# A four-layer graph network on one core: in the last layer, rows at run ends picked by one-hot products beside the groups, instead of a store of all rows and a second gather

## The reference, cut to what matters

```python
def _L3_gnn_ref(x, weight, bias, src, dst, rel):
    x_src = x[src]
    msg = zeros
    for r in range(4):
        hr = x_src @ weight[r] + bias[r]
        msg = where((rel == r)[:, None], hr, msg)
    agg = segment_max(msg, dst, num_segments=6250)
    agg = where((deg > 0)[:, None], agg, 0)
    return x @ weight[-1] + bias[-1] + agg

x = _layernorm(x + _L3_gnn_ref(x, ...))
```

## Time and profile before

| | |
|---|---|
| median of 3 runs | 4120.34 us |
| the profiled execution | 4121.19 us |
| its span, first to last instruction | 4119.4 us |
| PE / weight load busy in the span | 2465.8 / 2169.4 us |
| VectorE busy | 2245.0 us |
| ScalarE busy | 1038.2 us |
| POOL busy | 2912.2 us |
| granted TensorE clock, mean of the span | 0.632 of full speed |
| DMA | 602.65 MB, 147 GB/s over the span |

### The profile page before, as it was taken

How to read it: one execution, slowest core, us unless ns; L and a number is a source line. 1 busy time by engine, 2 the same in 40 slices (tenths; PEclk the granted TensorE clock), 3 DMA queues, 4 the chain that set the end, 5 groups by cost and what they waited for, 6 DMA issues and landing times. The chain is left out here.

```text
span 4119.4 us, 67476 instructions
## 1 busy us (share of the span) xinstructions
PE 2465.8 (60%) x18096; PEld 2169.4 (53%) x18096; DVE 2245.0 (54%) x6458; ACT 1038.2 (25%) x2890; POOL 2912.2 (71%) x3009
## 2 busy tenths in 40 slices
PE   2566666676647777529999977777633333333330
PEld 2454555454436666529999976666523333333330
DVE  5777777777744444436767668876522222222224
ACT  0244454444410111114444411111111111111112
POOL 2777777777747777626777777777377777777775
PEclk8555655656658898655555557767756556555655
DMA  4344444444425666446666678787545455444443
GB/s 121 97 113 129 116 132 128 117 130 115 130 71 144 146 147 147 80 95 176 183 182 176 185 217 262 249 246 250 178 122 130 129 134 132 129 132 132 130 129 94
DMA packets 454541, 602.65 MB, mean 146 GB/s; under 512 B 112602, under 2 KB 322350, under 8 KB 451086
## 3 DMA queue, kind: packets, MB, share of 16 engines
q1 hardware_dynamic: 344578, 392.09, 31.1%
q0 software_dynamic: 95744, 198.37, 22.2%
q10 hardware_dynamic: 14000, 9.82, 0.8%
HBM read 420.34 MB, written 184.16 MB: 147 GB/s over the span
## 5 line engine op out<-in xcount | busy, mean ns | idle before, releaser
L628 POOL DMA_INDIRECT G<-table,IC x2096 | 2002.2, 955 | 743.7 <-issue 633.3
L3342 DVE TENSOR_TENSOR_SCAN GW<-BIG,GW,PS 128x512 f32<-128x512 bf16 x208 | 266.2, 1280 | 781.6 <-PE PS L3317 766.8
L3317 PE MATMUL PS<-IDENT,G 128*128 128x128 f32 x832 | 204.2, 427 | 679.3 <-DMA G<-table,IC 679.3
L2936 POOL DMA_INDIRECT G<-table,IC x448 | 465.6, 1039 | 196.4 <-issue 139.0
L3317 PEld LDWEIGHTS PS<-IDENT,G 128*128 128x128 f32 x832 | 162.8, 223 | 717.7 <-DMA G<-table,IC 520.7
L2936 POOL DMA_INDIRECT G<-table2c,IC x384 | 369.8, 963 | 123.5 <-issue 116.2
L1284 PE MATMUL PS<-SEL,GW 128*128 128x96 f32 x1664 | 371.7, 414 | 78.1 <-DVEq L1360 78.1
L1284 PEld LDWEIGHTS PS<-SEL,GW 128*128 128x128 f32 x1664 | 347.2, 318 | 118.2 <-DVEq L1360 118.2
L2950 PE MATMUL PS<-BIG 128*128 128x49 f32 x1680 | 377.5, 412 | 1.1 <-ACT BIG L2885 1.1
L2950 PEld LDWEIGHTS PS<-BIG 128*128 128x128 f32 x1680 | 371.3, 333 | 1.3 <-ACT BIG L2885 1.3
L1162 ACT CAST BIG<-PS 128x490 bf16<-128x490 f32 x288 | 199.8, 706 | 257.1 <-PE PS L1149 252.4
(11 more groups left out here) (378 smaller groups left out, 4525.7 us busy)
## 6 DMA issues: line engine op xcount, KB each, us to landing
rows_ahead<-G SPq DMA_DIRECT2D x104, 520.0 KB
running_max<-BIG SPq DMA_DIRECT2D x105, 512.0 KB
GW<-source_in_block SPq DMA_DIRECT2D x160, 256.0 KB
G<-table,IC POOLq DMA_INDIRECT x2544
SCRATCH<-rows_ahead SPq DMA_DIRECT2D x78, 520.0 KB
SCRATCH<-edge_places SPq DMA_DIRECT2D x209, 192.0 KB
edge_counts<-BIG SPq DMA_DIRECT2D x24, 1568.0 KB
BIG<-run_mask SPq DMA_DIRECT2D x104, 256.0 KB
```

The source lines that it names most:

```text
L628: pool.indirect_dma_start(out=G[:, b, u, 0:width], out_offset=None, in_=table, in_offset=bass.IndirectOffsetOnAxis(ap=IC[:, b * U + u:b * ...
L2936: pool.indirect_dma_start(out=GS[:, b, u, 0:width], out_offset=None, in_=table, in_offset=bass.IndirectOffsetOnAxis(ap=IC[:, b * U + u:b * ...
L3317: last = t.transpose(PS[2 * q + u // 4][:, (u % 4) * P:(u % 4 + 1) * P], G[:, b, u, 0:D], IDENT[:])
L3342: v.tensor_tensor_scan(RM[:, q, h * 512:(h + 1) * 512], MB[:, q, h * 512:(h + 1) * 512], PS[2 * q + h][:], before, ALU.min, ALU.max).then_ ...
```

## The change

`edges3` and `finish` get a branch: they run only where `FLAG[0:1, 8:9]` is above 0 (`not_counted`). A new stage at the very end, `edges3_ends`, runs where it is below 1. The order of stages is now ..., rest2, edges3, exact3, finish, edges3_ends. The new stage has its loops written out for all 104 groups, but for POOL's, which stays a loop of 26 turns with the same gathers. For a group i:

- the gathers, transposes in, the scan, transposes back and the copies to RB are as before; RUNS is neither written nor read;
- VectorE compares `IOTA` with ENDREL (line 3624 of the new kernel): the edge's place in its window if it is the last edge of its run, else -1;
- TensorE multiplies: for each of the 8 tiles RB (edges x 128 features) by SEL (edges x 96), summed in PS6, so that each column is the one row at the end of that node's run (line 3588);
- VectorE adds the window to ACC (line 3646). Nodes without edges stay 0;
- at i = 12, 16, ..., 100 two node blocks are turned from ACC (line 3597), added to X and HS, and normalised over the next groups; SP stores them to `out`. The last 3 blocks follow the last group.

ENDREL comes ahead of the first group: SP loads the mask shifted by one edge, VectorE takes RELROW + 1 where the next edge starts a run, TensorE turns the 7 tiles of it, VectorE subtracts 1 and clears ACC (128 x 6368).

```diff
         def edges3():
...
                 @block.gpsimd
                 def _(pool):
+                    with pool.If(not_counted(pool)):
...
+        def edges3_ends():
...
+            def event(i, later):
+                n = (i - later) // RING - FIRST
+                return n if (i - later) % RING == 0 and 0 <= n < CHUNKS else None
...
+                def load_mask(sp, i):
+                    if i >= 2:
+                        sp.wait_ge(scanned, i - 1)
+                    sp.dma_start(MB[:, i % 2, :], MASKD[i * L:(i + 1) * L].unsqueeze(0)
+                                 .to_broadcast([P, L])).then_inc(mask_in[i % 2], 16)
...
+                def copy_back(act, i):
+                    q = i % 2
+                    act.wait_ge(back, i + 1)
+                    if i >= 2:
+                        act.wait_ge(picked, i - 1)
+                    a.copy(RB[:, q, 0:4, :], PS[4][:].rearrange("p (u f) -> p u f", u=4))
+                    a.copy(RB[:, q, 4:8, :], PS[5][:].rearrange("p (u f) -> p u f", u=4)).then_inc(copied, 1)
...
+                        for i in range(GROUPS + 1):
+                            if i < GROUPS:
+                                b = i % RING
+                                act.wait_ge(turned, i + 1)
+                                a.copy(IC[:, b * U:(b + 1) * U],
+                                       IDX3[:, (i + RING) * U:(i + RING + 1) * U]).then_inc(ic_ready, 1)
+                            if i >= 1:
+                                copy_back(act, i - 1)
+                            if event(i, 1) is not None:
+                                spread(act, event(i, 1))
+                            if event(i, 2) is not None:
+                                write_out(act, event(i, 2))
...
+                def turn_in(pe, i):
+                    b, q = i % RING, i % 2
+                    pe.wait_ge(gathered[b], i // RING * (16 * U) + 16 * U)
+                    if i >= 2:
+                        pe.wait_ge(scanned, i - 1)
...
+                def pick(pe, i):
+                    q = i % 2
+                    pe.wait_ge(copied, i + 1)
+                    pe.wait_ge(sel_ready, i + 1)
+                    if i >= 1:
+                        pe.wait_ge(added, i)
+                    for u in range(U):
+                        last = t.matmul(PS[6][:, 0:W], RB[:, q, u, :], SEL[:, q, u, :], start=u == 0, stop=u == U - 1)
+                    last.then_inc(picked, 1)
...
+                            if i < GROUPS:
+                                turn_in(pe, i)
+                            if i >= 1:
+                                turn_back(pe, i - 1)
+                            if i < GROUPS and event(i, 0) is not None:
+                                turn_nodes(pe, event(i, 0), i - 1)
+                            if i >= 1:
+                                pick(pe, i - 1)
+                        turn_nodes(pe, CHUNKS, GROUPS)
...
+                def select_ends(dve, i):
+                    if i >= 2:
+                        dve.wait_ge(picked, i - 1)
+                    v.tensor_tensor(SEL[:, i % 2], times(IOTA[:, 0:W], U), per(ENDREL[:, i * U:(i + 1) * U], W),
+                                    ALU.is_equal).then_inc(sel_ready, 1)
...
+                def mix_best(dve, cn, n):
+                    b0, nb = events[n]
+                    Y = X[:, b0:b0 + nb, :]
+                    dve.wait_ge(sums_turned, n + 1)
+                    cn.step(v.tensor_tensor(Y, rows(PS[7], nb), Y, ALU.add))
+                    dve.sem_inc(taken, 1)
+                    cn.step(v.tensor_tensor(Y, Y, HS[:, b0:b0 + nb, :], ALU.add))
...
+                        for i in range(GROUPS + 1):
+                            if event(i, 2) is not None:
+                                scale(dve, event(i, 2))
+                            if i < GROUPS:
+                                dve.reg_load([regs[i % 2]], BASE[0:1, i:i + 1])
+                                select_ends(dve, i)
+                                scan(dve, i)
+                            if i >= 1:
+                                add_ends(dve, regs[(i - 1) % 2], i - 1)
+                            if i < GROUPS and event(i, 0) is not None:
+                                mix_best(dve, cn, event(i, 0))
+                        mix_best(dve, cn, CHUNKS)
+                        scale(dve, CHUNKS)
```

More of the change, by code:

```diff
@@ L3257, in _ @@
                 def _(act):
[L3258 to L3269, removed]
@@ L3275, in _ @@
+                    act.nop()
                 @block.gpsimd
                 def _(pool):
[L3277 to L3281, removed]
+                    with pool.If(not_counted(pool)):
+                        with pool.Fori(0, LAPS) as turn:
+                            for b in range(RING):
+                                pool.wait_ge(ic_ready, turn * RING + b + 1)
+                                pass_wait(pool)
+                                gather_group(pool, T3, D, b, gathered)
@@ L3283, in _ @@
+                    pool.nop()
                 @block.sync
                 def _(sp):
[L3285 to L3296, removed]
@@ new lines, in turn_in, with turn_back @@
+                def turn_in(pe, i):
[3 more added lines that the diff above has]
+                        pe.wait_ge(scanned, i - 1)
+                    for u in range(U):
+                        last = t.transpose(PS[2 * q + u // 4][:, (u % 4) * P:(u % 4 + 1) * P], G[:, b, u, 0:D], IDENT[:])
+                    last.then_inc(turned, 1)
+                def turn_back(pe, i):
+                    q = i % 2
+                    pe.wait_ge(scanned, i + 1)
+                    if i >= 1:
+                        pe.wait_ge(copied, i)
+                    for u in range(U):
+                        last = t.transpose(PS[4 + u // 4][:, (u % 4) * P:(u % 4 + 1) * P],
+                                           RM[:, q, u * P:(u + 1) * P], IDENT[:])
+                    last.then_inc(back, 1)
@@ new lines, in pick, with turn_nodes @@
+                def pick(pe, i):
+                    q = i % 2
+                    pe.wait_ge(copied, i + 1)
+                    pe.wait_ge(sel_ready, i + 1)
+                    if i >= 1:
+                        pe.wait_ge(added, i)
+                    for u in range(U):
+                        last = t.matmul(PS[6][:, 0:W], RB[:, q, u, :], SEL[:, q, u, :], start=u == 0, stop=u == U - 1)
+                    last.then_inc(picked, 1)
+                def turn_nodes(pe, n, windows):
+                    b0, nb = events[n]
+                    pe.wait_ge(added, windows)
+                    if n >= 1:
+                        pe.wait_ge(taken, n)
+                    for j in range(nb):
+                        last = t.transpose(PS[7][:, j * P:(j + 1) * P], ACC[:, (b0 + j) * P:(b0 + j + 1) * P], IDENT[:])
+                    last.then_inc(sums_turned, 1)
@@ new lines, in _ @@
+                @block.tensor
+                def _(pe):
+                    with pe.If(is_counted(pe)):
+                        pe.wait_ge(ends_ready, 1)
+                        for g0, g1, bank in ((0, 4, 6), (4, TG, 7)):
+                            for grp in range(g0, g1):
+                                last = t.transpose(PS[bank][:, (grp - g0) * P:(grp - g0 + 1) * P],
+                                                   ENDROW[:, grp * P:(grp + 1) * P], IDENT[:])
+                        last.then_inc(ends_turned, 1)
+                        for i in range(GROUPS + 1):
[8 more added lines that the diff above has]
+                        turn_nodes(pe, CHUNKS, GROUPS)
+                    pe.nop()
```

347 lines of the change are left out of this document (257 added, 90 removed).

## The result

The changed kernel takes **4088.03 us** (median of 4 runs, 4084.37 to 4089.57) against 4120.49 for the kernel before on the same chip: ratio 0.992, 95% interval 0.9906 to 0.9934, or 32 us less. Forecast were 4096.0 and a range of 4064 to 4124. The profiled execution has a span of 4086.3 us (before 4119.4).

The account below looks back on a forecast made before the run. POOL's issue rate was taken to bound the edge stage. From the profiled 4121.2 us, -67.4 (tail), +11 (empty stages) and +32 (contention) gave 4096.8, or 4096.0 for the median of runs; range 4064 to 4124.

Parts of the forecast that it names:

- What bounds the kernel, and what is taken away: Last layer's edge stage: POOL's issue rate sets it, 10.0 us a group; all 92.9 us behind the last edge gather go.
- The stores at nothing: Edge stage: removing 105 stores of 512 KB gains nothing, since POOL does not wait for SP or the DMA engines.
- The new tail: Behind the last gather: landing, last group's work, last node blocks and end take 25.5 us; net gain 67.4 us.
- the middle: Tail from the last group's first transpose to ScalarE's end: 17.6 us.
- Rival D: Edge stage: a group's own chain grows beyond 10.0 us; each 0.5 us over costs 52 us, 4116 to 4170; chance 0.05.
- Empty stages: Ahead of the new stage: three stages passed empty at 3.3 us each, branch about 1: +11 us, bounds 7 and 13.
- The start of the stage: Opening of the new stage: two loads, two VectorE passes, 7 transposes and clearing ACC cost nothing.
- Added inside a group: Edge stage: only the two-SBUF comparison costs, holding up POOL 0.30 us a group; +32 us with the second node add.
- Rival B: Edge stage: every gather start inside a comparison waits, starts fall evenly; 0.46 us a group, 4113 us; chance 0.14.
- Rival C: Edge stage: comparison's phase against gathers fixed and bad, 0.55 to 0.8 us each; slower, 4138 at 0.7; chance 0.09.
- Rival A: Edge stage: comparisons miss POOL's gather starts, under 0.1 us a group; 4064, up to 4074 us; chance 0.20.
- E: New stage is not taken: one more empty stage and the branches, 4127 us; chance 0.01.

Follow-up runs that it names:

- experiment 8: Changed kernel with the 512 KB stores of turned rows to RUNS put back for 102 groups, read by nobody; 4092.58 us, ratio 0.9926.
- experiment 1: Changed kernel with each group's comparison reading the iota from a copy in PSUM instead of SBUF; 4065.35 us, ratio 0.9864.
- experiment 7: Changed kernel with the iota in PSUM and the three empty stages (edges3, exact3, finish) left out; 4063.1 us, ratio 0.9844.
- experiment 4: Changed kernel with a second two-SBUF-input comparison per group, ahead of the first, into memory nobody reads; 4105.57 us, ratio 0.9945.
- experiment 5: Changed kernel without the three stages passed empty ahead of the new one (edges3, exact3, finish); 4088.46 us, ratio 0.9917.
- experiment 6: Changed kernel with the iota in PSUM, and finish and edges3_ends called in one stage, one barrier less; 4069.93 us, ratio 0.9865.
- experiment 9: Changed kernel with the iota in PSUM and VectorE's end-list preparation held back until the first group of gathers landed; 4062.63 us, ratio 0.9858.
- experiment 2: Changed kernel with each group's comparison issued directly behind its scan instead of ahead of it; 4118.75 us, ratio 0.9984.

## Why the prediction was right, by its own steps

- **What bounds the kernel, and what is taken away.** Right: the stage kept POOL's pace, POOL waited 0.3 us for an index copy, and 92.9 us went. The stores at nothing: right for the stage, and within 1.7 us at the last landing (experiment 8).
- **The new tail.** It took 28.2 us instead of 25.5. The landing, 3.07 (forecast 3.0), and the end, 4.2 (4.9), were right; the middle was 20.9 (17.6). The failed step is "8 one-hot products for group 102, of a kind that takes 3.73 us for 16 when slow, so 1.9": the x16 in rows 6 counts records, and each of these f32 products leaves two. Eight products take 3.73 at 1.2 GHz and 2.02 at 2.4. The slip counts twice, 2 x (3.73 - 1.9) = 3.7 us, more than the middle's 3.3; it also put the group's end at T + 6.8 where it is T + 6.5 at the fast level (36 groups) and T + 8.6 at the slow (67). Rival D had 3 us of slack by that count and really 1.4. What the middle takes is left to the clock: 20.9 where both last sets of products were slow, 18.1 to 18.3 with one of them slow (experiments 1, 7 and 8), 16.0 to 16.3 with none (experiments 4, 5, 6 and 9). So a forecast of 17.6 with the slip in it could have come out right by luck.
- **Empty stages.** +8.6 for +11, within its bounds of 7 to 13; 2.6 each and 0.6 for the branch where I took 3.3 and 1. The price came from stages upstream; it is not one price for any stage.
- **The start of the stage.** "I cost this at nothing": off by 2.0 us. I asked who waits for the new VectorE passes, and not whom they hold up on the port.
- **Added inside a group.** The mechanism held in full: the same stage with the iota in PSUM loses the 24.6 us. The size was 24.6 for 32. Growing as its length, my first scaling gave 0.24 a group, which is what was measured, but that is luck. By the sum under experiment 2 a comparison whose starts are spread evenly costs 0.78 x 0.78 / 2 / 1.25 = 0.24 us (an estimate: the hold falls evenly from 0.78 to nothing over 0.78 of each 1.25 us), and one of 0.556 us costs 0.38 x 0.38 / 2 / 1.25 = 0.06: it grows faster than the square of the length. The short ones cost more than that in the stage of rows 7, where 19 of them hold a gather, by 5.8 us in all or 0.11 for each of the 54; they did not fall evenly there. The 0.30 a group is the term that was too large, by 6.
- **Rival B** (0.46 a group) had its condition nearly met, since the starts are spread, and its price wrong: it added the 0.13 us of a handover to what is left of the comparison, where the rows take 0.13 away. It is almost exactly the price in experiment 2 (0.48), by another reason: there the places cluster. The Trainium skill ("SBUF — State Buffer", section "SBUF: two separate sides") has the lock held for the whole instruction by whichever side is first, with about 115 ns behind VectorE's end. The trace agrees that a gather waits for the comparison. It agrees too, to within 0.05 us, that the first to start wins, as the two pairs under experiment 2 show. It differs in the other two. A held gather ends 0.82 us behind the comparison's end, less than the 0.94 of a free one; either 0.13 us of its own work lie ahead of the wait, or the wait ends before the comparison does, and nothing of the 115 ns is left over. And a gather doesn't keep VectorE out for its whole length: a comparison that starts 0.1 to 0.4 us into a running gather isn't delayed and holds nobody (at most 0.007 us on average, 36 cases). As far as these rows show, only a gather's start contends.
- **Rival C** named the right danger: a fixed distance between landing and comparison. Here the products' two speeds and the node pieces break it up. It needed 0.54 us a group to turn the sign, and the worst order tried had 0.48, which left a ratio of 0.9984.
- **Rival A** fell: the places are spread, not favourable. **D** and **E** did not come. (In the chances, E's 0.01 is counted as slower, though its 4127 lies among the same.)

The sum for the profiled execution: -64.7 for -67.4, +8.6 for +11, +25.3 for +32. It took 4088.2 us where 4096.8 were worked out, 8.6 less: 6.7 are the contention, 2.2 the untouched code upstream, and the dearer tail (2.7) is nearly paid by cheaper empty stages (2.4). The 2.2 are luck: in the twelve traces the last stores of the rest stage stand anywhere from 2974.9 to 2986.8, in code that is the same in all.

## What to carry to other kernels

Before adding VectorE work beside a gather stage that sets the pace, look where its inputs lie: the same comparison cost 24.6 us with both inputs in SBUF and held no gather with one of them in PSUM. If both must stay in SBUF, what counts is where it falls in POOL's period, so a move in the order of the code that looks harmless can double its price. And count the records of a kind of product against its lines of code before taking a duration from a row.

## What the runs showed of the hardware that I had not expected

- The hold depends on the place to a few hundredths of a microsecond: a 0.96 us comparison costs a 0.94 us gather with 0.30 us of issue between 0 and 0.78 us, linearly in how near to the gather's start it begins, and nothing once it begins less than 0.045 us ahead of it.
- A single-input f32 pass over 896 columns (0.56 us) holds a gather as well: 2.79 to 2.81 us for the first gather in eight kernels, 0.94 with that pass moved. That gather starts 1.43 us before the pass, and unhindered it would have been over 0.48 before it. The clearing of GW, 0.25 us ahead of the gather in both cases, doesn't hold it when the pass isn't queued behind it (experiment 9). So the pass holds the gather while it is still queued, or the two together do; which, stays open. That a hold passes on to an operation queued behind is in the trace of the kernel before as well, in 26 gathers, of which one:

```profile
1903.38 0.48 DVE L730 TENSOR_SCALAR SCRATCH<-SCRATCH,PART 96x1024 bf16<-96x1024 bf16 x1
1903.50 1.58 POOL L2936 DMA_INDIRECT G<-table,IC  x1 [0.30 <-issue]
1903.78 0.48 DVE L3039 TENSOR_SCALAR GW<-GW,PART 128x1024 bf16<-128x1024 bf16 x1
```

  The gather ends at 1905.08, 0.82 behind the end of the second pass, which began 0.28 after it.
- The barrier and the clearing of semaphores between two stages are 0.2 to 0.4 us; a stage passed empty costs 2.6 with them.
- The last group's landing, 3.07 us behind the last gather, is 1.7 later with the 512 KB stores put back.
